# Low-rank rows, B and C parts and layer-norm statistics in the prologue of a selective scan

## The reference

```python
# third block, the end: down projection, added to x
h = rms_norm(silu(bit_linear(x, w_gate)) * bit_linear(x, w_up), ln_weight)
x = x + bit_linear(h, w_down)
# fourth block, on x = layernorm(x)
xp = einsum('bld,ed->ble', x, Wx)                # 96 rows: 64 for dt, 16 for B, 16 for C
dt_x, B, C = xp[..., :64], xp[..., 64:80], xp[..., 80:]
dt = softplus(einsum('blr,dr->bld', dt_x, Wdt) + bdt)
A = -exp(A_log)
dA, dBx = exp(dt * A), dt * B * x                # per position, column and 16 states
# h = dA_t * h + dBx_t along 128 positions;  y_t = sum over states of h * C_t
return y + x * D
```

## Time and profile before

| | us |
|---|---|
| median of 3 runs | 1215.55 (1214.44 to 1221.83) |
| profiled execution: time | 1216.69 |
| profiled execution: span | 1214.9 |
| start of the statistics (L128) | 301.96 |
| start of the first dBx (L978) and of the last product with C (L987) in the loop | 340.29 and 491.40 |

### The profile page before, as it was taken

How to read it: one execution, slowest core, us unless ns; L and a number is a source line. 1 busy time by engine, 2 the same in 40 slices (tenths; PEclk the granted TensorE clock), 3 DMA queues, 4 the chain that set the end, 5 groups by cost and what they waited for, 6 DMA issues and landing times.

```text
span 1214.9 us, 15485 instructions
## 1 busy us (share of the span) xinstructions
PE 1015.3 (84%) x5192; PEld 644.1 (53%) x5202; DVE 836.2 (69%) x1392; ACT 619.5 (51%) x1493; POOL 494.6 (41%) x374
## 2 busy tenths in 40 slices
PE   5999879464646666358899999999999999999998
PEld 3777654223212222136667677777767565555554
DVE  4568639977699999767888877778787445332232
ACT  2445646066477663157778777687766223211111
POOL 0022277151056671137777765677654422100000
PEclk9878859778768787679999999999999999999999
DMA  9501130300100000000000014200003000000000
GB/s 334 243 1 51 69 139 0 125 32 5 24 0 1 0 0 0 2 1 1 2 1 2 1 45 126 70 2 1 2 1 122 1 1 1 1 18 1 1 1 18
DMA packets 24319, 43.78 MB, mean 36 GB/s; under 512 B 3616, under 2 KB 19936, under 8 KB 22624
## 3 DMA queue, kind: packets, MB, share of 16 engines
q1 hardware_dynamic: 24240, 42.79, 10.5%
HBM read 41.74 MB, written 1.05 MB: 35 GB/s over the span
## 4 chain that ended last, share of the span: by engine, by line
PE 58%; DVE 24%; ACT 10%; issue 5%; POOL 1%; DMA 1%; SPq 0%; DVEq 0%; ACTq 0%; POOLq 0%
PE ps L2165 12%; PE ps L2186 8%; DVE arena L982 6%; PE ps L1723 4%; PE ps L1736 4%; PE ps L1682 3%; DVE arena L978 3%; ACT arena L1027 3%; ACT ps L2011 3%; PE ps L1707 3%; PE ps L1690 3%; PE ps L437 2%; PE ps L400 2%; PE ps L1715 2%; PE ps L1697 2%
## 5 line engine op out<-in xcount | busy, mean ns | idle before, releaser
L2204 DVE TENSOR_TENSOR arena<-arena,ps 128x512 f32<-128x512 f32 (+1 forms) x56 | 38.5, 687 | 146.0 <-ACT arena L2197 143.9
L2089 POOL TENSOR_TENSOR arena<-arena 128x4 f32<-128x4 f32 x96 | 99.0, 1032 | 47.3 <-DVE arena L1839 44.5
L2197 ACT ACTIVATE arena<-ps,arena 128x512 f32<-128x512 f32 (+1 forms) x56 | 38.4, 686 | 156.0 <-PE ps L2165 156.0
L1061 PE MATMUL ps<-arena,ident 128*128 128x512 f32 x128 | 82.6, 781 | 37.6 <-DVE arena L987 37.6
L2186 PE MATMUL ps<-wide,arena 128*128 128x256 f32 (+1 forms) x448 | 106.3, 380 | 0.0
L2011 ACT ACTIVATE ps<-ps,arena 128x128 f32<-128x128 f32 x256 | 88.4, 355 | 28.3 <-DVE arena L1818 28.3
L2003 ACT ACTIVATE arena<-ps,arena 128x512 f32<-128x512 f32 x96 | 68.1, 784 | 65.9 <-PE ps L1697 65.8
L2186 PEld LDWEIGHTS ps<-wide,arena 128*128 128x128 f32 (+1 forms) x448 | 84.7, 190 | 17.9 <-issue 1.8
L2165 PE MATMUL ps<-XT,wide 128*128 128x512 f16 (+1 forms) x384 | 93.3, 379 | 0.0
L1818 DVE TENSOR_REDUCE arena<-ps 128x4 f32<-128x512 f32 x64 | 43.8, 690 | 47.5 <-PE ps L1707 47.4
L1690 PE MATMUL ps<-wide,arena 128*128 128x512 f16 x256 | 66.6, 397 | 11.2 <-POOL arena L2069 9.1
(11 more groups left out here) (322 smaller groups left out, 2469.1 us busy)
## 6 DMA issues: line engine op xcount, KB each, us to landing
side<-in_wproj SPq DMA_DIRECT2D x1, 4096.0 KB, 14.2
wide<-in_w_down SPq DMA_DIRECT2D x1, 3584.0 KB, 13.9
side<-in_w_gate SPq DMA_DIRECT2D x1, 3520.0 KB, 30.8
side<-in_w_up SPq DMA_DIRECT2D x1, 3520.0 KB, 12.1
wide<-in_w_gate SPq DMA_DIRECT2D x2, 1728.0 KB, 11.9
side<-in_w_up SPq DMA_DIRECT2D x3, 1024.0 KB, 9.3
arena<-in_taps SPq DMA_DIRECT2D x1, 2048.0 KB, 13.6
wide<-in_wq SPq DMA_DIRECT2D x1, 2048.0 KB, 10.7
```

Of the source, the lines that this page charges most:

```text
L1061: last = pe.matmul(ps[:, 4 + 2 * c + j, :], k.ident[:, :], read[i % 2][:, 512 * j:512 * j + 512], start=(n == 0), stop=(n == NST - 1), ski ...
L2089: pool.tensor_tensor(rs[:, j, :], var[:, j, :], minus_half[:, j, :], ALU.pow).then_inc(rs_ready, 1)
```

## The change

Only names of semaphores change outside `ffn` and `scan` (three are merged or dropped in `cross` and in the expert block, with the same waits), and a constant array is no longer loaded. In `ffn`'s last loop DVE takes the statistics of batch b - 1 (L137, L138) before it waits for the down projection of batch b, so that the scan's norm has one batch left. In `scan`:

- Wx, Wdt, bdt, D and A_log are loaded once the block before `ffn` has ended; `pick`, now 96 x 32 x 128, is built by GpSimd from the identity (two additions of 96x32, one cast of 96x4096) right after its last `ffn` instruction.
- ACT copies to `XT` before it takes the root of the totals; ACT negates the decay itself.
- The low-rank rows come from one matmul for all 96 rows, in two halves of 512 tokens (4 matmuls); ACT copies dt's rows out for each half.
- B and C (32 rows) are cut together, straight from PSUM, at the same time as dt's rows are worked on; one cut of 6 DVE instructions stands for two of 5.
- Abs waits for dt's matmul alone, before DVE's max; Abs and Exp alternate by column half; the second dt * x stands behind the first step.

```diff
@@ -762,6 +762,8 @@
         for b in range(B):
             if b + 2 < B:
                 quantise(b + 2)
+            if b:
+                k.early_stats(dve, link, b - 1, added)
     dt = A.take([KC, N])
     dtx = A.take([KC, N])
     dA = [A.take([N]) for _ in range(2)]
-    pick_raw = Arena(k.arena, A.at).take([NST, P])
     dBx = [A.take([N]) for _ in range(2)]
     state = [A.take([N]) for _ in range(2)]
     read = [A.take([N]) for _ in range(2)]
 
 
-    b_rows, c_rows = A.take([N]), A.take([N])
-    b_parts, c_parts = A.take([N], BF16), A.take([N], BF16)
-    pick = A.take([NST, P], BF16)
+    parts = A.take([N], BF16)
+    unsplit = [A.take([k.proj.SPLIT]), k.XN[:, 0:k.proj.SPLIT // D, :].rearrange("p b d -> p (b d)")]
+    A = Arena(k.arena, 15080)
     wx = A.take([KC, DTR + 2 * NST])
-    wdt = A.take([D])
     bdt, dskip = A.take([KC]), A.take([KC])
     decay = A.take([KC, NST])
-    unsplit = [A.take([k.proj.SPLIT]), k.XN[:, 0:k.proj.SPLIT // D, :].rearrange("p b d -> p (b d)")]
-    assert A.at <= 18688, A.at
+    one = A.take([2 * NST])
+    assert A.at <= 15360, A.at
+    pick = Arena(k.arena, 15360).take([2 * NST, P], BF16)
+    wdt = Arena(k.arena, 18432).take([D])
     w = k.proj
     dt_rows = state[1]
-    middle = state[0][:, 0:N // 2].bitcast(BF16)
-    K3 = 64 + NST
-    tmp = [dA[0], dA[1]]
+    R0, R1 = DTR, DTR + 2 * NST
+    K3 = 3 * 2 * NST
+    rest = state[0][R0:R1, :]
+    high = state[1][R0:R1, 0:N // 2].bitcast(BF16)
+    middle = state[1][R0:R1, N // 2:].bitcast(BF16)
+    tmp = [read[0], read[1]]
     acc = k.XN.rearrange("p b d -> p (b d)").rearrange("p (c n) -> p c n", c=KC)
 
...
@@ -927,52 +932,47 @@
         return ps[:, i:i + 2, :].rearrange("p a b -> p (a b)")
 
     def sync(sp):
-        sp.wait_ge(k.x_done, 3)
-        for dst, src in ((pick_raw[0:K3], a["pick"].rearrange("k (n p) -> k n p", n=NST)),
-                         (wx, a["Wx"].rearrange("(c p) n -> p c n", p=P)), (wdt[0:DTR], a["Wdt"]),
+        sp.wait_ge(k.x_done, 2)
+        for dst, src in ((wx, a["Wx"].rearrange("(c p) n -> p c n", p=P)), (wdt[0:DTR], a["Wdt"]),
                          (bdt, a["bdt"].rearrange("p c o -> p (c o)")),
                          (dskip, a["D1"].rearrange("p c o -> p (c o)")),
                          (decay, a["A_log"])):
             sp.dma_start(dst, src).then_inc(w_loaded, 16)
 
     def vector(dve, link):
-        k.norm_vector(dve, link, 4)
+        k.norm_vector(dve, link, 4, early=B - 1)
         w.total_vector(dve, link)
-        dve.wait_ge(decay_exp, 1)
-        link(dve.tensor_scalar(decay, decay, -1.0, None, ALU.mult))
-        dve.sem_inc(decay_ready, 1)
-        dve.memset(b_parts[0:K3], 0.0)
-        link(dve.memset(c_parts[0:K3], 0.0))
-        dve.wait_ge(w_loaded, 96)
-        link(dve.tensor_copy(pick[0:K3], pick_raw[0:K3]))
-
-        def cut(rows, parts, low):
-            dve.wait_ge(low_ready, low)
-            rows, mid = rows[0:NST, :], middle[0:NST, :]
-            link(dve.tensor_copy(parts[0:NST, :], rows))
-            link(dve.tensor_tensor(rows, rows, parts[0:NST, :], ALU.subtract))
-            dve.tensor_copy(parts[32:32 + NST, :], rows)
-            link(dve.tensor_copy(mid, rows))
-            link(dve.tensor_tensor(parts[64:64 + NST, :], rows, mid, ALU.subtract))
-            dve.sem_inc(parts_ready, 1)
-
-        cut(b_rows, b_parts, 2)
-
-        for c in range(KC):
-            dve.wait_ge(dt_psum, c + 1)
-            dve.tensor_scalar(dt[:, c, :], banks(2 + 2 * c), bdt[:, c:c + 1], 0.0, ALU.add,
-                              ALU.max).then_inc(dt_relu, 1)
-        cut(c_rows, c_parts, 3)
-        for c in range(KC):
+        for t in dA:
+            last = dve.memset(t.rearrange("p (b s) -> p b s", s=S)[:, :, 0:1], 0.0)
+        link(last)
+
+        def softplus(c):
             dve.wait_ge(dt_log, c + 1)
             dve.wait_ge(dt_relu, c + 1)
             dve.tensor_tensor(dt[:, c, :], dt[:, c, :], tmp[c], ALU.add).then_inc(dt_ready, 1)
+
+        def scaled(c):
             dve.wait_ge(dt_ready, c + 1)
             link(dve.tensor_tensor(dtx[:, c, :], dt[:, c, :], k.XT[:, c, :], ALU.mult))
-        for t in dA:
-            last = dve.memset(t.rearrange("p (b s) -> p b s", s=S)[:, :, 0:1], 0.0)
-        link(last)
+
+        dve.wait_ge(low_psum, 2)
+        rows = banks(6)[R0:R1, :]
+        link(dve.tensor_copy(high, rows))
+        link(dve.tensor_tensor(rest, rows, high, ALU.subtract))
+        link(dve.tensor_copy(middle, rest))
+        dve.tensor_copy(parts[0:2 * NST, :], high)
+        dve.tensor_copy(parts[2 * NST:4 * NST, :], middle)
+        dve.tensor_tensor(parts[4 * NST:6 * NST, :], rest, middle, ALU.subtract).then_inc(parts_ready, 1)
+        for c in range(KC):
+            dve.wait_ge(dt_abs, c + 1)
+            dve.tensor_scalar(dt[:, c, :], banks(2 + 2 * c), bdt[:, c:c + 1], 0.0, ALU.add,
+                              ALU.max).then_inc(dt_relu, 1)
+        softplus(0)
+        softplus(1)
+        scaled(0)
         for i, (n, c) in enumerate(STEPS):
+            if i == 1:
+                scaled(1)
             dve.wait_ge(b_psum, n + 1)
             wait(dve, state_ready, i - 1)
             dve.tensor_tensor(dBx[i % 2], dtx[:, c, :], banks(0), ALU.mult).then_inc(dBx_ready, 1)
@@ -1002,24 +1002,21 @@
 
     def scalar(act, link):
         k.norm_scalar(act, 4)
+        k.turn_scalar(act, 2)
         w.root(act)
-        k.turn_scalar(act, 2)
-        act.wait_ge(w_loaded, 96)
-        act.activation(decay, decay, ACT.Exp).then_inc(decay_exp, 1)
-        act.wait_ge(low_psum, 1)
-        act.copy(dt_rows[0:DTR, :], banks(4)[0:DTR, :]).then_inc(low_ready, 1)
-        act.wait_ge(low_psum, 2)
-        act.copy(b_rows[0:NST, :], banks(6)[0:NST, :]).then_inc(low_ready, 1)
-        act.wait_ge(low_psum, 3)
-        act.copy(c_rows[0:NST, :], banks(0)[0:NST, :]).then_inc(low_ready, 1)
+        act.wait_ge(w_loaded, 80)
+        link(act.activation(decay, decay, ACT.Exp))
+        link(act.activation(decay, decay, ACT.Copy, scale=-1.0))
+        for j in range(2):
+            act.wait_ge(low_psum, j + 1)
+            act.copy(dt_rows[0:DTR, 512 * j:512 * j + 512], ps[0:DTR, 6 + j, :]).then_inc(low_ready, 1)
         for c in range(KC):
-            act.wait_ge(dt_relu, c + 1)
-            link(act.activation(tmp[c], banks(2 + 2 * c), ACT.Abs, bias=bdt[:, c:c + 1]))
-        for c in range(KC):
+            act.wait_ge(dt_psum, c + 1)
+            act.activation(tmp[c], banks(2 + 2 * c), ACT.Abs, bias=bdt[:, c:c + 1]).then_inc(dt_abs, 1)
+            act.wait_ge(dt_abs, c + 1)
             link(act.activation(tmp[c], tmp[c], ACT.Exp, scale=-1.0))
         for c in range(KC):
             act.activation(tmp[c], tmp[c], ACT.Ln, bias=1.0).then_inc(dt_log, 1)
-        act.wait_ge(decay_ready, 1)
         for i, (n, c) in enumerate(STEPS):
             if i < 2:
                 act.wait_ge(dt_ready, i + 1)
@@ -1032,25 +1029,26 @@
 
     def tensor(pe):
         k.turn_tensor(pe, 3, 2)
-        pe.wait_ge(w_loaded, 96)
-        pe.wait_ge(k.xt_ready, 12)
-        for m0, m, bank in ((0, DTR, 4), (DTR, NST, 6), (DTR + NST, NST, 0)):
-            for j in range(2):
-                for c in range(KC):
-                    last = pe.matmul(ps[0:m, bank + j, :], wx[:, c, m0:m0 + m], k.XT[:, c, 512 * j:512 * j + 512],
-                                     start=(c == 0), stop=(c == KC - 1))
+        pe.wait_ge(w_loaded, 80)
+        for j in range(2):
+            pe.wait_ge(k.xt_ready, 10 + 2 * j)
+            for c in range(KC):
+                last = pe.matmul(ps[0:R1, 6 + j, :], wx[:, c, :], k.XT[:, c, 512 * j:512 * j + 512], start=(c == 0),
+                                 stop=(c == KC - 1))
             last.then_inc(low_psum, 1)
-        pe.wait_ge(low_ready, 1)
         for c in range(KC):
             for j in range(2):
+                if c == 0:
+                    pe.wait_ge(low_ready, j + 1)
                 last = pe.matmul(ps[:, 2 + 2 * c + j, :], wdt[0:DTR, c * P:(c + 1) * P],
                                  dt_rows[0:DTR, 512 * j:512 * j + 512], start=True, stop=True)
             last.then_inc(dt_psum, 1)
-        def spread(n, rows, bank, done, free):
+
+        def spread(n, first, bank, done, free):
 
             wait(pe, free, KC * n)
             for j in range(2):
-                last = pe.matmul(ps[:, bank + j, :], pick[0:K3, n, :], rows[0:K3, 512 * j:512 * j + 512],
+                last = pe.matmul(ps[:, bank + j, :], pick[0:K3, first + n, :], parts[0:K3, 512 * j:512 * j + 512],
                                  start=True, stop=True)
             last.then_inc(done, 1)
 
@@ -1062,18 +1060,16 @@
                                  start=(n == 0), stop=(n == NST - 1), skip_group_check=True)
             last.then_inc(summed, 1)
 
-        pe.wait_ge(low_ready, 3)
+        pe.wait_ge(pick_ready, 3)
         pe.wait_ge(parts_ready, 1)
-        spread(0, b_parts, 0, b_psum, dBx_ready)
```

(34 more changed lines are left out.)

2 lines of the change are left out of this document (removed).

## The result

| comparison | changed kernel, us | kernel before, us | ratio, 95% interval |
|---|---|---|---|
| first | 1200.11 (1195.47 to 1201.22, 4 runs) | 1216.99 (1214.44 to 1221.83, 4 runs) | 0.9849 [0.9808, 0.9891] |
| repeat, 5 rounds | 1199.58 (1197.88 to 1201.57, 5 runs) | 1214.43 (1211.2 to 1219.21, 11 runs) | 0.9873 [0.9852, 0.9894] |

The change makes the kernel faster by 1.3 to 1.5%. The forecast was 1203.8. So the direction held and the forecast gain was too small: 15 to 18 us were gained where 11.8 were forecast. That much is clear of the spread, since the intervals reach up to 1202.3 and 1202.7 and no higher. On which side of the range's low end the kernel lies is not: the two comparisons disagree on it.

The account below looks back on a forecast made before the run. The latency of the chain of waits from 298 to 350 us, no single engine, was taken as the bound. 15.2 - 0.2 - 3.2 = 11.8 us off the median 1215.55 gave 1203.8, range 1199.5 to 1208.

Parts of the forecast that it names:

- The prologue: Scan, from the statistics' start to the second scan instruction's end: 48.1 us to fall to 32.9, a gain of 15.2.
- T: Zero point of the forecast's times: the start of the statistics for the scan's norm, 301.96 us in the profile before.
- The cut of B and C: VectorE's cut in the scan, from T + 9.15 to T + 14.6, hidden under ACT's 17.9 with 0.8 us to spare.
- The one slow and seven fast low-rank instructions: TensorE's 8 low-rank instructions in the scan: one at about 0.85 us, seven at 0.43, done at T + 9.1.
- the loop's entry: First scan steps: GpSimd's pieces delay the second dt * x to T + 28.5 and the second scan to T + 32.9.
- The 2.5: At the first scan steps: 2.5 us more gain if the collisions with GpSimd fell away.
- The pick matrix: GpSimd's cast of 3.8 us at the end of ffn makes L749 on VectorE wait; cost 3.2 us (2.6 to 4.0).
- no port wait: Rival: L749 in ffn does not wait for GpSimd's cast; gain 15.0, so 1200.5 us; chance 0.10.
- slow cast: Rival: GpSimd's step-0 cast runs element by element, a loss beyond 15.6 us; at 5 ns an element 1220.9; chance 0.03.
- The early statistics: Seven batches' statistics in ffn's last loop cost 0.2 us at the last quantise, bounds 0 and 0.6.
- behind the loop all shifts alike: After the scan's loop everything moves by the same amount; the clock may fall elsewhere, left at 1 us either way.

Follow-up runs that it names:

- root first: Changed kernel with ScalarE's root of the totals put ahead of the copies to XT again; 1200.93 us, one run.
- whole rows: Changed kernel without token halves: TensorE waits for all four copies, ACT copies dt's rows out once; 1202.06 us, one run.
- the pieces from step 3: Changed kernel with pick built later and GpSimd's weight pieces begun at loop step 3 instead of 0; 1196.03 us, ratio 0.9857 to the kernel before.

## Why the prediction was too small

**The prologue: the mechanism and nearly the size.** Measured against the same trace of before, 48.07 - 31.92 = 16.15 us, forecast 15.2. The steps, as forecast and as found, from T:

| step | forecast | found |
|---|---|---|
| XN starts | 1.2 | 1.25 |
| low-rank rows done | 9.1 | 8.9 |
| dt's second half done | 12.8 | 12.5 |
| first Ln done | 17.9 | 17.7 |
| max of both halves done | 17.1 | 16.8 |
| first scan ends | 25.2 | 24.8 |
| second dt * x ends | 28.5 | 27.8 |
| second scan ends | 32.9 | 31.9 |

The cut of B and C, at T + 14.3, was hidden as forecast, and Ln was the last to free softplus: VectorE waits 0.86 us for it. The one slow and seven fast low-rank instructions came true in this trace, and partly by luck: over the traces of the changed kernel and its variants the eight took 3.60 (all fast) to 3.99.

Only at the loop's entry was the size off. The pieces on GpSimd in the changed kernel (timeline):

```profile
328.12 3.43 POOL L1256 TENSOR_TENSOR wide<-arena,wide 128x1024 f16<-128x1024 f32 x1 [29.51 <-ACT wide L1250]
331.52 3.11 POOL L1256 TENSOR_TENSOR wide<-XN,wide 128x1024 f16<-128x1024 f32 x1
```

The order was as forecast: the first scan holds the first piece, that piece holds the second dt * x, this holds the second piece, and that one the second scan. But the pieces ended at 331.55 and 334.63, and the product and the scan lost 0.62 and 0.56. The forecast named 2.5 for the two. That is more than its own marks give: the product with C (L987) stands ahead of the second dt * x, so by them the waits are about 0.9 and 0.85. The 2.5 does not enter the 15.2.

**The pick matrix.** Cost 2.5, forecast 3.2. The mechanism was right (L749, beside the cast, until its end). The cast took 3.59 instead of 3.8, its two additions 0.25 instead of 0.4 each, so it started sooner behind GpSimd's last product, and L749 met it 0.93 us after its start instead of 0.58. Reading one number 128 times over with step 0 is no slower here than the casts of the earlier trace rows, whose pace gives 3.8. The rival "no port wait" fell, and so did "slow cast". The Trainium skill's rule (SBUF — State Buffer, Who interferes with whom) holds here with 2.68 us, and the estimate of 6.1 for the cast from its GPSIMD Engine Reference, section 3.1, does not: 3.59.

**The early statistics.** Forecast 0.2, found nothing: 21.38 us from L753 to T with them and without.

**The step that failed** is, above all, "behind the loop all shifts alike; the clock there may fall elsewhere, which I leave at 1 us either way". VectorE runs 13.25 us ahead of the kernel before all through the loop, but behind it 15.45, so the term put at nothing, 1 us either way, measured 2.2. The last sums and the transposes, 3.21 and 3.35 in both traces of the kernel before, took 1.98 and 1.97 in both of the changed kernel. This is before (timeline of TensorE),

```profile
492.68 3.21 PE L1061 MATMUL ps<-arena,ident 128*128 128x512 f32 x4 [2.73 <-DVE arena L987]
497.26 3.35 PE L1081 MATMUL ps<-ident,XN 128*128 128x128 f32 x16 [1.37 <-DVE XN L993]
```

and this is after:

```profile
479.41 1.98 PE L1059 MATMUL ps<-arena,ident 128*128 128x512 f32 x4 [1.23 <-DVE arena L987]
482.77 1.97 PE L1077 MATMUL ps<-ident,XN 128*128 128x128 f32 x16 [1.38 <-DVE XN L993]
```

The granted clock over these four stretches (busy time by stretch), before,

```profile
492.68:495.89 3.21, 3.20 (x4) 0.88 (x4) 1.13 (x1) 0.00 (x0) 0.00 (x0) 0.60 0.00 0
497.26:500.61 3.35, 3.34 (x16) 3.10 (x16) 1.87 (x3) 0.00 (x0) 0.00 (x0) 0.57 0.00 0
```

and after:

```profile
479.41:481.39 1.98, 1.98 (x4) 0.68 (x4) 1.14 (x1) 0.00 (x0) 0.00 (x0) 1.00 0.00 0
482.77:484.74 1.97, 1.97 (x16) 1.74 (x16) 1.27 (x3) 0.00 (x0) 0.00 (x0) 1.00 0.00 0
```

Sums and transposes both stand in the chain, with VectorE waiting. The edit has no part in their code; it only moved them in time, to where the clock was at 2.4 GHz. That this part of the gain came is luck: of the eleven traces of the changed kernel and its variants, five had the tail fast throughout. How loosely it is tied is in the table: 0.8 us at the prologue (root first) lost 2.1 in the tail, and so did moving the pick matrix, while 3.3 us (whole rows) lost nothing. The bound should have been 2 us or more to either side.

**The base.** The sum was made against one execution, and against its longest prologue and its lower clock in ffn. In the first pair of traces the misses are: pick matrix 0.7, early statistics 0.2, clock in ffn 1.1, prologue 0.95, tail and loop 2.2; with the 11.8 that is 16.9, what was measured from ffn on. Against the second trace of before the prologue gains 14.2 and ffn costs 2.7, and with the tail's 2.1 it is 13.9. On that trace the same forecast gives 46.07 - 32.9 = 13.2 for the prologue and 9.8 in all, so it is too small by 4.1, and the tail is again the largest part. The repeated comparison, 0.9873 or 15.4 us, lies between.

**What stays open** is what sets the clock's level in the tail. That its length follows the level is seen in the two traces above; that TensorE's share in the loop decides it was tried, and the two traces don't support it. In what share of executions either kernel meets the high level there, these 14 traces don't tell.

## What to carry to other kernels

In a chain of short steps on several engines, sum the steps one by one from rows of the same shape, the collisions too; here that held within a microsecond of 48. Before an idle GpSimd is given work, look for the small VectorE products beside it: one of eight numbers waited 2.5 us for the end of a 3.59 us cast. A collision in which GpSimd starts second cost the VectorE instruction nothing here, but the held-up piece ends later and may then hold the next one: 0.62 us in the changed kernel, nothing with the pieces from step 3. Take two traces of the kernel before wherever TensorE's clock swings, and widen the range by each later stretch of matmuls in the chain that may meet the other level.
